# Second attention's gating and expert weights moved from VectorE to GpSimd, first attention's maxima transposed by VectorE

## The chip, the cores and the metric

The kernel runs on one core of a Trainium2 chip. TensorE (PE; PEld is its weight load), VectorE (DVE), ScalarE (ACT), GpSimd (POOL) and SyncE (SP, which here only issues DMAs) each run their own instruction list in order and meet at semaphores. The metric is the device time of one execution in microseconds, as the median of repeated runs.

## What is computed

`x` is [32, 256, 128] in float32, 8192 tokens. Layer 0 adds a latent attention with 16 heads and a top-1 mixture of 8 experts. Layer 1 adds a second attention (16 heads; a local window of 32, a remote part over 64 pooled latents, each scaled by a gate) and a mixture of 64 experts, top 8, with a shared expert.

```python
xn = _layernorm(x)
x = x + _L0_attn_ref(xn, ...) + _L0_ffn_ref(xn, ...)
xn = _layernorm(x)
x = x + _L1_attn_ref(xn, ...) + _L1_ffn_ref(xn, ...)

# _L0_attn_ref: a softmax over causal scores of width 36
scores = jnp.einsum('bhtl,bsl->bhts', q, Wdkv) / sqrt(d_head)
attn = jax.nn.softmax(jnp.where(causal, scores, -inf), axis=-1)
# _L1_attn_ref: the gates
gl = jax.nn.sigmoid(jnp.einsum('bhsd,hd->bhs', Q, gate_local_w))[..., None]
gr = jax.nn.sigmoid(jnp.einsum('bhsd,hd->bhs', Q, gate_remote_w))[..., None]
out = gl * local + gr * rem
# _L1_ffn_ref: the weights of the experts
w, idx = jax.lax.top_k(softmax(x @ gate_w), 8)
w = w / jnp.sum(w, axis=-1, keepdims=True)
shared = shared * jax.nn.sigmoid(x @ shared_gate_w)
```

## The kernel before

Each engine's list is written by hand, and the order of the calls is the order of the work. A batch is 256 tokens; there are 32, numbered by pair and half, and buffers alternate by half. The stages follow one another: the first attention (to about 830 us of the profile), the top-1 experts (to 985), the second attention and the routing (to 1600), the 64 experts.

First attention. One step handles the probabilities of batch b, the maxima and queries of the next batch n, and the keys of m after that. `smax` on TensorE (L1786 to L1799) makes scores of n in bfloat16 only to find each row's maximum; `red` on VectorE (L904 to L908) reduces them into `mneg`, eight pairs of heads a batch. `mt` then turns `mneg` [128 tokens, 16 heads] into rows: two transposes on TensorE (L1805) into `bankA`, a copy by ScalarE into `mT` (L1460), and two DMAs on SP that write `mT` into row 36 and row 100 of `qT` (`maxima`, L358 to L362), so that the real score matmul `st` (L1815, L1818) subtracts the maximum itself. `st(b, 0)` waits for these DMAs. TensorE ends a step with `smax(n, 7)`, `av(b, 3)`, `mt(n)`, `kv(m)`, `qproj(m, 0)`, and opens the next with `outp` (L1845, L1847) and `st`. On SP `maxima` stands ahead of `denominators` (L364 to L386): `remainders<-yT` (L367), then, once it has landed, `dq<-remainders` (L369). VectorE inverts `dq` (`invert`, L912) between `red(n, 0)` and `red(n, 1)`.

Second attention. One step handles the softmax and result of b, the projection and routing of n, the layer norm of m, and the combination of p, the batch before b. VectorE's order (`step1`, L1301) is: `pool_latents(n)` (L1216, `xp`), `shift(b,1)`, `combine(p)` (L1289 `at1`, L1291 `at2`, L1293 `aT`), `turn(b,0)`, `shift(b,2)`, `finish(p)`, `turn(b,1)`, `route(n)` (L1226 to L1234), `sums1(m)`, `shift(b,3)`, `turn(b,2)`, `mean1(m)` (L1211, `mv`), `turn(b,3)` (L1264), `weigh(n)` (L1240 to L1247), `shared_gated(b)` and `shared_hidden(b)` (L1270, L1275, into `shT`), `invert1(b)` (L1279), `shift(n,0)`, `turn_rows(b)` (L1283, `rowsT`). ScalarE goes from `xt1` (L1557, `xT`) over `keys(n)` (L1571 to L1575), `latent_keys(n)` (L1590 to L1595) and the exponentials (L1552) to `attended(b)`, which copies `rows` out of PSUM (L1634 to L1639). GpSimd adds the layer-0 experts to the stream and normalises (`stream1`, `norm1`), divides the rows (`normalise_rows`, L818), adds the residual (L786) and gathers rows for a later batch (L767). TensorE ends a step with `attend(b, 2)`, `attend(b, 3)`, `scores(n, 0)`, `shared_down(b)` (L2115), `scores(n, 1)`, `xt1(m)` (L2021) and `remote(b)` (L2107), which reads `rowsT`, and opens the next with `qk(n)` (L2030).

Of the kernel before, what the change touches and what calls it, by code (L numbers as in the profile page):

```python
# [9 lines left out]
ALU = mybir.AluOpType  # L10
ACT = mybir.ActivationFunctionType
AX = mybir.AxisListType
P = 128
NEG = -1e30
# [3 lines left out]
class Batch:  # L18
# [8 lines left out]
    def before(self):  # L27
        return Batch(self.pair, 0) if self.half == 1 else Batch(self.pair - 1, 1)

# [4 lines left out]
def program(nc, a, out):  # L34
# [27 lines left out]
    with ctx:  # L62
# [112 lines left out]
        mneg = sb("mneg", [P, 2, 2, 2, PAIRS])  # L175
        mT = sb("mT", [H, 2, T])
# [39 lines left out]
        lg1 = sb("lg1", [P, 2, E1 + 1])  # L216
        mx8 = sb("mx8", [P, 2, 8])
        lgr = sb("lgr", [P, 2, E1])
        mb = sb("mb", [P, 2, 2, E1], BF16)
        shl = sb("shl", [P, 2, E1])  # L220
        exl = sb("exl", [P, 2, E1])
# [77 lines left out]
        names = """consts zeroed zeroed1 w_a w_in x_in0 x_in1 x_in2 x_in3 bn stats_done var rstd_done xn_done xn_got xnT_ps  # L299
        xt_ps xt_act xt_dve rk_sb scats xnT_sb kv_ps kv_sb  # L300
        q_ps q_sb s_ps red_done mT_ps mT_sb st_ps exp_done av_done y_sb den_out den_in rec_done rec_out zrows_in z_done out_ps xa_done cst dumped passed xs_zero rt ex0 rk_ps staged scat0 scat1 te_done xs_in0 xs_in1 w1_sb xsT_ps xsT_sb h_ps h_act h_dve
# [3 lines left out]
        sh1_done sh_sb shd_ps av_ps rd_done rows_turned rem2_ps v_out v_in0 v_in1 rows_sb gate_ps gate_sb comb aT_done scaled x1_copied ao_ps r1_done res_done  # L305
        tab_out0 tab_out1 res_out0 res_out1 l1_consts wprep xpr_sb slots cnt_out cnt_in0 cnt_in1 owner_done picked_ps sel sidx_done tokf_done diag_done row_done same_done first_done mg_done ym_sb xg_in0 xg_in1 
# [20 lines left out]
        def _(sp):  # L327
# [82 lines left out]
            sp.dma_start(gw[:, 0:E1], a["L1_ffn_gate_w"]).then_inc(S["w1_in"], 16)  # L410
            sp.dma_start(gw[:, E1:E1 + 1], a["L1_ffn_shared_gate_w"]).then_inc(S["w1_in"], 16)
# [122 lines left out]
        def _(pool):  # L534
# [74 lines left out]
            def layer1_masks(g):  # L609
# [7 lines left out]
                if g == 3:  # L617
                    pool.memset(maskl[:, 0, 0:W], NEG).then_inc(S["l1_consts"], 1)
                    pool.wait_ge(S["l1_consts"], 1)
# [150 lines left out]
            def stream1(n):  # L770
# [6 lines left out]
                pool.wait_ge(S["x1_done"], n.b * 2 + 1)  # L777
# [17 lines left out]
            def norm1(n, prior):  # L795
# [5 lines left out]
                pool.wait_ge(S["x1_done"], n.b * 2 + 2)  # L801
                passed(pool)
                pool.tensor_copy(tab[:, u, :, 0:C], xa_all[:, bass.ds(n.b * 2, 2), :]).then_inc(S["x1_copied"], 1)
                deviation(n)
                pool.wait_ge(S["x1_copied"], n.b + 1)
# [15 lines left out]
            gather(Batch(0, 0))  # L821
            gather(Batch(0, 1))
            clear()
            stream1(Batch(0, 0))
            norm1(Batch(0, 0), False)
            stream1(Batch(0, 1))
            norm1(Batch(0, 1), False)
            gather(Batch(1, 0))
            with pool.Fori(0, LOOP - 1) as i:
                for b in (Batch(i, 0), Batch(i, 1)):  # L830
                    stream1(b.next().next())
                    norm1(b.next().next(), True)
                    normalise_rows(b)
                    add_stream(b)
                    gather(b.next().next().next())
            stream1(Batch(LOOP, 0))
            norm1(Batch(LOOP, 0), True)
            normalise_rows(Batch(LOOP - 1, 0))
# [42 lines left out]
        def _(dve):  # L881
# [140 lines left out]
            def step(n, p, q, staged, prior=True):  # L1022
# [20 lines left out]
                if n:  # L1043
                    red(n, 7)
# [1242 lines left out]
```

## Time and profile before

| | us |
|---|---|
| median of 3 runs | 1768.62 (1762.4 to 1772.06) |
| the profiled execution | 1777.13 |
| its span | 1774.3 |

| engine | busy us | share of the span |
|---|---|---|
| PE | 1545.6 | 87% |
| VectorE | 1153.1 | 65% |
| ScalarE | 1004.9 | 57% |
| GpSimd | 833.2 | 47% |

The span is cut into 40 slices of 44 us on the profile's page. TensorE shows 9 tenths or more in nearly all slices up to 830 us, and VectorE shows 9 tenths from 1020 to 1600 us. The granted TensorE clock is at full speed in both attentions and falls to 6 to 7 tenths at the end.

### The profile page before, as it was taken

The page shows a single profiled execution, that of the slowest core. Times are in us where ns is not written, and L with a number is a line of the kernel's source. Part 1 is how long each engine was busy: PE and PEld are TensorE (multiplying, and loading weights), DVE is VectorE, ACT ScalarE, POOL GpSimd, SP SyncE. Part 2 cuts the span into 40 slices and gives each one's busy share as a digit, 9 for nine tenths or more (in the row PEclk, how much of TensorE's full clock was granted, in tenths as well). Part 3 has the DMA queues.
Part 4 walks back from the last instruction along what each step waited for, and adds up shares of the span by engine and source line. Part 5 has one row for each costly group of instructions (what it writes and reads, how often), then busy time and mean ns, then how long its engine had stood idle before and what let it go on. Part 6 is the DMA issues. An engine that isn't in the chain of part 4 may idle for free.

```text
span 1774.3 us, 44513 instructions
## 1 busy us (share of the span) xinstructions
PE 1545.6 (87%) x14114; PEld 1125.7 (63%) x14115; DVE 1153.1 (65%) x2767; ACT 1004.9 (57%) x2558; POOL 833.2 (47%) x1415
## 2 busy tenths in 40 slices
PE   4798999999999999998998588888888888875883
PEld 4655555555555555555998477777777777764672
DVE  3355555555555555543554499999999999986661
ACT  3344555555555555543332578888788887862331
POOL 5233555555555555554443544444444444412663
PEclk9998999999999999999999599999999999996666
DMA  7402222222222222223332121111211212116444
GB/s 194 131 17 66 55 55 55 55 55 55 55 55 55 55 55 55 55 58 71 70 71 58 23 46 41 42 44 43 44 39 42 44 43 44 39 34 123 85 84 116
DMA packets 237550, 107.52 MB, mean 61 GB/s; under 512 B 141625, under 2 KB 225914, under 8 KB 237434
## 3 DMA queue, kind: packets, MB, share of 16 engines
q1 hardware_dynamic: 227258, 93.23, 21.9%
q0 software_dynamic: 10240, 13.64, 3.6%
q8 instruction: 27, 0.44, 0.1%
q14 instruction: 25, 0.20, 0.0%
HBM read 61.92 MB, written 40.16 MB: 58 GB/s over the span
## 4 chain that ended last, share of the span: by engine, by line
PE 49%; DVE 21%; issue 12%; DMA 6%; ACT 4%; SPq 3%; POOL 2%; DVEq 1%; POOLq 0%; another core or an unknown queue 0%; ACTq 0%
PE bankB L1832 7%; PE bankA L1780 5%; DVE mxs L1254 5%; DVE pt L1264 5%; PE bankT L1815 5%; PE bankT L1967 4%; PE bankB L1836 3%; PE bankS L1793 3%; PE bankT L1818 2%; PE bankB L2115 2%; DMA remainders<-yT 2%; PE bankS L1956 2%; PE bankT L1956 2%; PE bankB L1845 2%; DMA dq<-remainders 2%
## 5 line engine op out<-in xcount | busy, mean ns | idle before, releaser
L667 POOL TENSOR_SCALAR_AFFINE_SELECT probs<-probs 128x512 f32<-128x512 f32 x256 | 183.2, 739 | 167.0 <-ACT probs L1464 167.0
L906 DVE TENSOR_REDUCE mneg<-bankS 128x2 f32<-128x256 f32 x256 | 107.6, 420 | 227.2 <-PE bankS L1798 196.5
L1464 ACT ACTIVATE probs<-bankT 128x1024 f32<-128x1024 f32 x128 | 131.0, 1023 | 189.9 <-PE bankT L1818 189.9
L907 DVE TENSOR_REDUCE mneg<-bankS 128x2 f32<-128x512 f32 x256 | 174.6, 682 | 0.0
L1455 ACT ACTIVATE qT<-bankA,bd 128x256 f32<-128x256 f32 x256 | 107.5, 473 | 91.7 <-PE bankA L1780 91.7
L1780 PE MATMUL bankA<-xnT,wd 128*128 128x256 f32 x512 | 151.2, 420 | 0.0
L1815 PE MATMUL bankT<-qT,kT 37*128 37x512 f32 x512 | 140.0, 623 | 7.5 <-DMA qT<-mT 5.7
L660 POOL CAST qb<-qT 128x256 bf16<-128x256 f32 x256 | 97.2, 398 | 100.7 <-ACT qT L1455 100.5
L1832 PE MATMUL bankB<-probs,vaug 128*64 128x512 f32 x512 | 141.5, 631 | 1.1 <-ACT yT L1471 1.0
L1264 DVE STREAM_TRANSPOSE pt<-pe 128x768 f32<-128x768 f32 x128 | 123.7, 966 | 0.9 <-ACT pe L1552 0.9
L1471 ACT COPY yT<-bankB 128x512 f32<-128x512 f32 x128 | 75.0, 586 | 85.4 <-PE bankB L1836 85.4
L1780 PEld LDWEIGHTS bankA<-xnT,wd 128*128 128x128 f32 x512 | 90.8, 197 | 38.1 <-issue 30.4
L1552 ACT ACTIVATE pe<-pr 128x768 f32<-128x768 f32 x128 | 108.1, 845 | 10.4 <-DVE pr L1258 6.5
L2086 PE MATMUL bankT<-vx,pt 128*64 128x68 f32 x1024 | 72.1, 227 | 42.0 <-ACT gkm L1595 42.0
L1818 PEld LDWEIGHTS bankT<-qT,kT 37*128 37x128 f32 x512 | 51.1, 192 | 63.1 <-issue 63.1
L1793 PEld LDWEIGHTS bankS<-rowneg,rowsel 64*128 64x128 bf16 x1024 | 36.2, 95 | 84.7 <-issue 45.5
L2086 PEld LDWEIGHTS bankT<-vx,pt 128*64 128x64 f32 x1024 | 55.3, 136 | 54.4 <-ACT gkm L1595 27.5
L1836 PEld LDWEIGHTS bankB<-probs,vaug 128*64 128x64 f32 x512 | 37.6, 140 | 75.5 <-issue 66.5
L767 POOL DMA_INDIRECT yg<-ys_sorted,idx_g x64 | 67.2, 1049 | 36.9 <-POOL gate_g L763 26.7
L1793 PE MATMUL bankS<-rowneg,rowsel 64*128 64x128 bf16 x1024 | 74.9, 223 | 10.6 <-DVE mneg L907 6.8
L730 POOL COPY probs<-wall 128x516 f32 x72 | 44.8, 623 | 77.2 <-DVE qT L1138 74.3
L1818 PE MATMUL bankT<-qT,kT 37*128 37x256 f32 x512 | 79.0, 386 | 0.0
(316 smaller groups left out, 4301.9 us busy)
## 6 DMA issues: line engine op xcount, KB each, us to landing
rzb<-reciprocals SPq DMA_DIRECT2D x128, 128.0 KB
yT<-yT SPq DMA_DIRECT2D x64, 128.0 KB
xtab<-tab SPq DMA_DIRECT2D x32, 192.0 KB, 2.0
xs_sorted<-zeros SPq DMA_DIRECT2D x1, 4608.0 KB, 18.6
qT<-xs_sorted SPq DMA_DIRECT2D x144, 32.0 KB, 1.8
ys_sorted<-qT SPq DMA_DIRECT2D x36, 128.0 KB, 1.9
value_rows<-vrow SPq DMA_DIRECT2D x32, 128.0 KB, 1.8
vx<-value_rows SPq DMA_DIRECT2D x256, 16.0 KB, 1.8
```

Source lines behind the costliest of these rows:

```text
L667: pool.affine_select(out=blocks, in_=blocks, compare_op=ALU.is_ge, fill=0.0, base=0, pattern=[[0, 4], [1, P]], channel_multiplier=-1).then ...
L906: dve.tensor_reduce(mneg[:, n.half, 0, :, j], bankS[:, :, 0:128], AX.X, ALU.max, negate=True)
L907: dve.tensor_reduce(mneg[:, n.half, 1, :, j], bankS[:, :, 128:384], AX.X, ALU.max, negate=True).then_inc(S["red_done"], 1)
L1264: dve.transpose(pt[:, g].rearrange("p k b g q -> p (k b g q)"), pe1[:, g % 2].rearrange("p k s q -> p (k s q)")).then_inc(S["tr_done"], 1)
L1464: act.activation(pT[:, g % 2].rearrange("p e j t -> p e (j t)"), bankT[:, 0:2, :], ACT.Exp, scale=SCALE0).then_inc(S["exp_done"], 1)
L1552: act.activation(pe1[:, g % 2].rearrange("p k s q -> p s k q"), pr[:, g % 2, :].rearrange("p (s k q) -> p s k q", k=2, q=W), ACT.Exp, scal ...
L1780: ins = pe.matmul(bankA[:, k * T:(k + 1) * T], wd[:, 2 * r + k, :, :].rearrange("p e l -> p (e l)"), xnT[:, n.half, :], start=True, stop=True)
L1793: pe.matmul(blocks, rowsel[HALVES[e], k, :], rowneg[HALVES[e], k, :].unsqueeze(1).to_broadcast([LP, 2, LP]), start=(k == 0), stop=False, s ...
L1815: pe.matmul(bankT[:, e, :], kT[KEYS[e], u, 0:P], qT[KEYS[e], u, 2 * g:2 * g + 2, :].rearrange("p j t -> p (j t)"), start=True, stop=True, ...
L1818: ins = pe.matmul(bankT[:, 2 + e, 0:T], kT[KEYS[e], u, P:T], qT[KEYS[e], u, 2 * g:2 * g + 2, P:T], start=True, stop=True, skip_group_check ...
L1832: pe.matmul(bankB[HALVES[e], :], vaug[:, u, 0, :], pT[:, g % 2, e].rearrange("p j t -> p (j t)"), start=True, stop=False, skip_group_check ...
L2086: pe.matmul(slots_ps[DL * k:DL * (k + 1), n, 0:PW], pt[:, g, 1, k, 2 * (n % 2):2 * (n % 2) + 2, :].rearrange("p g q -> p (g q)"), vx[:, u, ...
```

## The change

It takes `mt` off TensorE and ScalarE: VectorE transposes `mneg` in blocks of 32 by 32 right after `red(n, 7)`, and SP writes the result into `qT` with four DMAs (32 partitions of 128 bytes each) in place of two (8 partitions of 1 KB each). In the second attention VectorE's product for `at1` goes to GpSimd (`open_gate`, `local_gate`), and so do the mask product, the scaling of the shared gate and the final weights (`weigh`, `weights`). VectorE keeps the sum of the weights, over the eight largest logits that now sit behind the 64 in `lg1`, `shl` and `exl`. VectorE's `shift(b, 3)` goes ahead of `sums1(m)`. `pool_latents` is not touched; VectorE pools the latents before and after. Left out below: renamed semaphores and the same order in the opening and closing steps.

```diff
-        mneg = sb("mneg", [P, 2, 2, 2, PAIRS])
-        mT = sb("mT", [H, 2, T])
+        mneg = sb("mneg", [P, 2, 2, PAIRS, 2])
+        mT = sb("mT", [P, 2, 2 * H])
...
-        lg1 = sb("lg1", [P, 2, E1 + 1])
+        lg1 = sb("lg1", [P, 2, 1 + E1 + 8])
...
             def maxima(n):
                 sp.wait_ge(S["mT_sb"], n.b + 1)
-                for e in range(2):
-                    r = LP * e + L
-                    sp.dma_start(qT[r:r + 1, n.half], mT[PAIRS * e:PAIRS * (e + 1), n.half, :]).then_inc(S[f"m_in{n.half}"], 16)
+                for k in range(P // W):
+                    sp.dma_start(qT[L:LP + L + 1:LP, n.half].rearrange("e j (t k q) -> e (j t) k q", t=2, q=W)[:, :, k],
+                                 mT[W * k:W * (k + 1), n.half, :]).then_inc(S[f"m_in{n.half}"], 16)
...
+            def local_gate(b):
+                pool.wait_ge(S["gate_up"], b.b + 1)
+                pool.wait_ge(S["rows_turned"], b.b + 1)
...
+                pool.tensor_tensor(at1[:, :], tg[:, b.half, 0, :], rowsT[:, 0:T], ALU.mult).then_inc(S["local_done"], 1)
+
+            def open_gate(b):
+                gate = tg[:, b.half, 0, :]
+                pool.wait_ge(S["gate_sb"], b.b + 2)
...
+                pool.tensor_scalar(gate, gate, 1.0, None, ALU.add).then_inc(S["gate_up"], 1)
+
+            def weigh(n):
+                u = n.half
+                pool.wait_ge(S["ex_done"], n.b + 1)
+                pool.wait_ge(S["M_done"], n.b + 1)
...
+                pool.tensor_scalar(sgc[:, u, :], tsg[:, :], 0.5, 0.5, ALU.mult, ALU.add)
+                pool.tensor_tensor(exl[:, :, 0:E1], exl[:, :, 0:E1], mb[:, u], ALU.mult).then_inc(S["rstep"], 1)
+
+            def weights(n):
+                u = n.half
+                pool.wait_ge(S["rstep"], n.b + 1)
+                pool.wait_ge(S["wsum_done"], n.b + 1)
...
+                pool.tensor_tensor(tab[:, u, :, C:C + E1], exl[:, :, 0:E1], wsum[:, 1, :].unsqueeze(2).to_broadcast([P, 2, E1]),
+                                   ALU.mult).then_inc(S["tab_done"], 1)
+
+            def step1(b, n, m, k):
+                if m:
+                    stream1(m)
+                    copy1(m, True)
+                if n:
+                    weigh(n)
+                if m:
+                    norm1(m)
+                if n:
+                    weights(n)
+                if b:
+                    open_gate(b)
                     normalise_rows(b)
                     add_stream(b)
...
+                if b:
+                    local_gate(b)
+                if k:
+                    gather(k)
...
+            def turn_maxima(n, prior):
+                dve.wait_ge(S["red_done"], n.b * PAIRS + PAIRS)
...
+                dve.transpose(mT[:, n.half, :], mneg[:, n.half].rearrange("p e j t -> p (e j t)")).then_inc(S["mT_sb"], 1)
...
+            def weight_sum(n):
                 dve.wait_ge(S["ex_done"], n.b + 1)
...
+                dve.tensor_reduce(wsum[:, 0, :], exl[:, :, E1:E1 + 8], AX.X, ALU.add).then_inc(S["top8"], 1)
+                dve.wait_ge(S["top8"], n.b * 2 + 2)
+                dve.reciprocal(wsum[:, 1, :], wsum[:, 0, :]).then_inc(S["wsum_done"], 1)
...
             def turn_rows(b):
                 dve.wait_ge(S["scaled"], b.b + 1)
+                if not b.opens():
+                    dve.wait_ge(S["local_done"], b.b)
...
             def combine(b):
                 u = b.half
                 dve.wait_ge(S["gate_sb"], b.b + 2)
-                dve.wait_ge(S["rows_turned"], b.b + 1)
-                dve.scalar_tensor_tensor(at1[:, :], tg[:, u, 0, :], 1.0, rowsT[:, 0:T], ALU.add, ALU.mult).then_inc(S["comb"], 1)
                 dve.wait_ge(S["rem2_ps"], b.b + 1)
                 dve.scalar_tensor_tensor(at2[:, :], tg[:, u, 1, :], 1.0, rem_ps, ALU.add, ALU.mult).then_inc(S["comb"], 1)
-                dve.wait_ge(S["comb"], b.b * 2 + 2)
+                dve.wait_ge(S["comb"], b.b + 1)
+                dve.wait_ge(S["local_done"], b.b + 1)
                 dve.tensor_tensor(aT[:, :], at1[:, :], at2[:, :], ALU.add).then_inc(S["aT_done"], 1)
...
+                if b:
+                    shift(b, 3)
                 if m:
                     sums1(m)
                 if b:
-                    shift(b, 3)
                     turn(b, 2)
...
                 av(b, GROUPS - 1, True)
-                if n:
-                    if m:
-                        pe.wait_ge(S["xnT_sb"], m.b + 1)
-                    mt(n)
                 if m:
+                    pe.wait_ge(S["red_done"], n.b * PAIRS + PAIRS)
                     kv(m)
-                    pe.wait_ge(S["mT_sb"], n.b + 1)
                     qproj(m, 0)
```

## Rows read from the trace of the kernel before

**Rows 1.** Stretches: length, busy PE, PEld, DVE, ACT, POOL, granted clock, DMA, GB/s.
```profile
132.00:734.00 602.00, 589.49 (x4601) 340.37 (x4598) 326.25 (x678) 321.75 (x581) 301.76 (x527) 0.99 0.21 56
1026.00:1581.00 555.00, 483.05 (x6000) 404.54 (x6000) 529.39 (x1137) 452.11 (x1381) 256.40 (x409) 1.00 0.20 43
```

**Rows 2.** Timeline of a first-attention step: start, length, engine, line, operation.
```profile
441.34 0.68 DVE L907 TENSOR_REDUCE mneg<-bankS 128x2 f32<-128x512 f32 x1
...
442.41 0.39 PE L1805 MATMUL bankA<-ident,mneg 128*16 128x128 f32 x2
...
442.63 0.60 PE L1771 MATMUL bankS<-xnT,lw 128*128 128x256 f32 x2
...
443.38 1.38 SPq L362 DMA_DIRECT2D qT<-mT  x2
...
444.89 0.73 SPq L367 DMA_DIRECT2D remainders<-yT  x2
...
446.70 0.30 PEld L1815 LDWEIGHTS bankT<-qT,kT 37*128 37x128 f32 x4
```

**Rows 3.** Chain that ended last, first attention: start, length, what.
```profile
243.56 0.35 SPq L367
243.96 2.68 DMA remainders<-yT
246.65 2.29 DMA dq<-remainders
```

**Rows 4.** Who waited for whom, TensorE, 200 to 700 us: total, times, longest.
```profile
PE bankS L1793 <- DVE mneg L907: 3.4, 19, 0.3
```

**Rows 5.** SP's DMA instructions by line: minimum, median, maximum in ns.
```profile
L362 SPq DMA_DIRECT2D qT<-mT x64: 626/654/703, 93.6 to 806.0; - x64
...
L374 SPq DMA_DIRECT2D yT<-yT x64: 536/583/593, 126.3 to 830.9; - x64
```

**Rows 6.** The view of DMAs: kilobytes of each, median us from issue to landing.
```profile
vx<-value_rows SPq DMA_DIRECT2D x256, 16.0 KB, 1.8
```

**Rows 7.** Chain that ended last, an opening step of the first attention.
```profile
121.05 1.90 DMA qT<-mT
```

**Rows 8.** Timeline of a second-attention step, VectorE.
```profile
1205.57 0.96 DVE L1264 STREAM_TRANSPOSE pt<-pe 128x768 f32<-128x768 f32 x1
1206.45 0.25 DVE L1240 TENSOR_TENSOR exl<-exl,mb 128x128 f32<-128x128 f32 x1
...
1207.67 0.67 DVE L1270 SCALAR_TENSOR_TENSOR shT<-tsh,bankA 128x512 f32<-128x512 f32 x1
...
1211.15 0.57 DVE L1283 STREAM_TRANSPOSE rowsT<-rows 128x384 f32<-128x384 f32 x1
...
1214.22 0.42 DVE L1289 SCALAR_TENSOR_TENSOR at<-tg,rowsT 128x256 f32<-128x256 f32 x1
```

**Rows 9.** The same step, the other engines.
```profile
1207.10 1.57 POOL L809 TENSOR_SCALAR tab<-tab,mv,rstd 128x128 f32<-128x128 f32 x2 [0.21 <-POOL rstd L793]
1210.04 0.85 POOL L818 TENSOR_TENSOR rows<-rows,recd 128x384 f32<-128x384 f32 x1 [1.38 <-ACT rows L1639]
...
1211.77 0.71 PE L2107 MATMUL bankT<-rowsT,wro 128*128 128x128 f32 x4 [0.19 <-DVE rowsT L1283]
1212.32 1.03 PE L2030 MATMUL bankB<-xT,wqk 128*128 128x256 f32 x4
...
1213.38 0.37 ACT L1571 COPY qs<-bankB 128x256 f32<-128x256 f32 x1 [0.36 <-PE bankB L2030]
```

**Rows 10.** Who waited for whom in the second attention, 1026 to 1562 us: TensorE, GpSimd.
```profile
PE bankT L2086 <- ACT gkm L1595: 39.6, 29, 1.6
...
POOL rstd L791 <- DVE mv L1211: 124.9, 29, 4.4
```

**Rows 11.** Groups of GpSimd's instructions by line: busy us, mean ns, idle before.
```profile
L786 POOL TENSOR_TENSOR res<-res,xa_all 128x256 f32<-128x256 f32 x32 | 23.2, 726 | 11.0 <-ACT res L1623 10.8 <-issue 0.2
...
L775 POOL TENSOR_SCALAR yg<-yg,gate_g 128x128 f32<-128x128 f32 x64 | 38.3, 601 | 54.5 <-DMA yg<-ys_sorted,idx_g 54.5
```

More of the change, by code:

```diff
@@ L28, in before, with opens @@
         return Batch(self.pair, 0) if self.half == 1 else Batch(self.pair - 1, 1)
+    def opens(self):
+        return type(self.pair) is int and self.b == 0
     def two_before(self):
@@ L819, in normalise_rows @@
                                    ALU.mult).then_inc(S["scaled"], 1)
[L821 to L832, printed above, removed]
+            def local_gate(b):
+                pool.wait_ge(S["gate_up"], b.b + 1)
+                pool.wait_ge(S["rows_turned"], b.b + 1)
+                if not b.opens():
+                    pool.wait_ge(S["aT_done"], b.b)
+                passed(pool)
+                pool.tensor_tensor(at1[:, :], tg[:, b.half, 0, :], rowsT[:, 0:T], ALU.mult).then_inc(S["local_done"], 1)
@@ L845, in _ @@
-            normalise_rows(Batch(LOOP, 0))
-            add_stream(Batch(LOOP, 0))
-            normalise_rows(Batch(LOOP, 1))
-            add_stream(Batch(LOOP, 1))
+                if b:
+                    local_gate(b)
+                if k:
+                    gather(k)
+            first, second = Batch(0, 0), Batch(0, 1)
+            gather(first)
+            gather(second)
+            clear()
+            stream1(first)
+            copy1(first, False)
+            norm1(first)
+            step1(None, first, second, Batch(1, 0))
@@ new lines, in _ @@
+            step1(first, second, Batch(1, 0), Batch(1, 1))
+            step1(second, Batch(1, 0), Batch(1, 1), Batch(2, 0))
+            with pool.Fori(1, LOOP - 1) as i:
+                step1(Batch(i, 0), Batch(i, 1), Batch(i + 1, 0), Batch(i + 1, 1))
+                step1(Batch(i, 1), Batch(i + 1, 0), Batch(i + 1, 1), Batch(i + 2, 0))
+            step1(Batch(LOOP - 1, 0), Batch(LOOP - 1, 1), Batch(LOOP, 0), Batch(LOOP, 1))
+            step1(Batch(LOOP - 1, 1), Batch(LOOP, 0), Batch(LOOP, 1), None)
@@ L1075, in _ @@
             red(first, 7)
+            turn_maxima(first, False)
             best()
@@ L1082, in _ @@
                     onehot(j + 1)
+            turn_maxima(second, False)
             kv(Batch(1, 0))
@@ L1326, in step1 @@
                 if n:
-                    weigh(n)
+                    weight_sum(n)
                 if b:
@@ L1511, in _ @@
             xnt(second)
-            mt(first)
             qevac(second, 0)
@@ L1656, in step1 @@
                     values(n, b is not None)
-                    route(n)
+                    route(n, b is not None)
                 if b:
@@ L1799, in smax @@
                 ins.then_inc(S["s_ps"], 1)
-            def mt(n):
-                pe.wait_ge(S["red_done"], n.b * PAIRS + PAIRS)
-                passed(pe)
-                for t in range(2):
-                    ins = pe.transpose(bankA[0:H, t * P:(t + 1) * P], mneg[:, n.half, t].rearrange("p e j -> p (e j)"), ident[:, :])
-                ins.then_inc(S["mT_ps"], 1)
             def st(b, g, prior):
```

120 lines of the change are left out of this document (54 added, 66 removed).

## The prediction

> **What bounds the kernel now.** I read the busy time by stretch first, then the waits, then the timeline of one step in each attention, following what each engine waited for. In the first attention TensorE is busy 98% of the time at full clock [rows 1]; in the second VectorE is busy 95% and TensorE 87% [rows 1]. Both shares mislead.
>
> First attention. The step in rows 2 is 22.27 us long; steps run to 22.4 on average. TensorE's only wait is that `smax(n, 2)` waits for `red(n, 1)`, 19 times in 22 steps, 3.4 us in all, 0.18 us each [rows 4]. Behind it stands SP: the maxima's DMAs, `remainders<-yT`, 2.68 us in flight, `dq<-remainders`, 2.29 us, then `invert`, which VectorE runs ahead of `red(n, 1)` [rows 3]. So two chains are level within 0.2 us: TensorE's own work, and SP's chain, which starts when the maxima are turned.
>
> Second attention. The step is 18.45 to 18.5 us. VectorE runs from `turn(b,3)` at 1205.57 to `turn_rows` at 1211.15 without a gap [rows 8]. TensorE's `remote` waits for `rowsT` (0.19 us), `qk` follows it, and ScalarE's `qs` waits for `qk` [rows 9]. From `qs` ScalarE runs on to `gkm`, for which TensorE's `attend` waits 29 times [rows 10]; TensorE then runs on to the end of `attend(b,3)`, ScalarE copies `rows`, GpSimd divides them, and `turn_rows` needs that. GpSimd ends at 1210.89 (1210.04 + 0.85, itself released by ScalarE's rows) and `turn_rows` starts at 1211.15 [rows 8, 9]. This is the number that matters most: only 0.26 us after its operand is there does VectorE reach the instruction. In alternate steps of the timeline it is 0.30. VectorE is the last comer by a quarter of a microsecond, and behind it a second closed ring (`qs`, `gkm`, `attend`, `rows`, division, turn, `remote`, `qk`, `qs`) has nearly the same period.
>
> **The change part by part, second attention.** Off VectorE: `weigh` takes 1.22 us (1206.45 to 1207.67) [rows 8]. What stays is a sum over 16 elements and a reciprocal, about 0.35, so 0.87 goes. `at1` is 0.42 long [rows 8], 0.33 from start to start. `shift(b,3)` ahead of `sums1(m)` hides a gap of about 0.1 behind a long instruction. `shl` grows from 64 to 72 columns, 0.02 back. Sum 1.3 us off a VectorE step. Of this only `weigh` lies between `turn(b,3)` and `turn_rows`: VectorE would reach `turn_rows` 0.87 earlier, but its operand is only 0.26 to 0.30 early, less about 0.04 for a release (`turn_rows` ended at 1211.72, `remote` began at 1211.77 [rows 8, 9]). The gain is 0.22 to 0.26 us a step; the rest becomes VectorE idling at `turn_rows` and before `turn(b,3)`, where it waits for ScalarE's last exponential. Some 29 steps: 7 us.
>
> This holds if GpSimd's division still starts when `rows` come. Ahead of it now stand `weights` and `open_gate`. `norm1` ended at 1208.67 and the division began at 1210.04, 1.37 us later [rows 9]; and since VectorE now has time over, `mean1`, for which GpSimd waits (124.9 us in 29 steps [rows 10]), comes up to 0.7 us earlier in the ring, so there are 1.4 to 2.0 us. `weights` is a product of 128 columns: 0.73 for 256 [rows 11] gives 0.4 to 0.5. `open_gate` adds a constant to 256 columns, a form the trace does not show at this size; below it stands half the 0.73 of the two-input product, above it the 0.60 for 128 columns with a pointer scalar doubled, 1.2 [rows 11]. I take 1.0, from the nearer form. Together 1.4 to 1.5: it fits, barely at the upper end without the earlier `mean1`. `weigh` (0.7) falls into the 4.4 us in which GpSimd waited for `mean1` [rows 10]. `local_gate` (0.73 by `res` [rows 11]) waits for `turn_rows`; queued behind it is `gather`, whose rows are then some 0.5 us later, against 2 us in which `x1_done` is early. `aT` needs `at1` only after `shift(b,1)` and `at2`, over 2 us after `turn_rows`; no cost. `tab` is saved 1.3 us later; SP is then still issuing value rows. No cost.
>
> **First attention.** Off TensorE: `mt`, 0.22 us from its start at 442.41 to `kv` at 442.63 [rows 2]. Off ScalarE a copy that hid. On VectorE a transpose of 32 columns, 0.2 by the slope between 384 columns (0.57) and 768 (0.96) [rows 8], plus 0.16 for the wait on its own semaphore. `red` ends at 442.02 [rows 2], so `mT` is ready at 442.4 instead of 443.36; that is 0.95 earlier. Then SP issues four DMAs instead of two. With a cost c per issue, `remainders<-yT` starts at 442.41 + 4c + 0.13, before at 444.89 [rows 2]: later by 4c - 2.35. The pair L362 took 1.38, so c = 0.69; L374, the other copy from SBUF to SBUF and like the new ones from 32 partitions, has a median of 0.58, 0.60 from start to start [rows 5]. Smaller issues on this queue exist (0.36 for L367 [rows 2]). Bounds 0.36 to 0.69; I take 0.60, since L374 is the nearest form: later by 0.05. So SP's chain, which carries the step, stays where it was, and TensorE's 0.22 goes into its wait for `red(n,1)`, which grows from 0.18 to about 0.4. Steady gain between -0.05 and +0.05 a step, 0 us. In the opening steps `st` waited for the maxima themselves, and `mt` stood alone on the path: 1 to 1.5 us gained. The maxima for `st(b,0)`: last issue at 442.41 + 1.8, landing 1.90 later [rows 7], at 446.1, against 446.70 - 0.22 [rows 2]: in time. The 128-byte pieces: the `vx` DMAs move 64-byte pieces and land 1.8 us after issue [rows 6], so I add nothing. `normalise(p, 2)` is 0.3 later on VectorE, a microsecond before `outp` needs it.
>
> **Sum.** 7 + 1.3 = 8.3 us off 1777.13 of the profiled execution (span 1774.3). The median is 8.5 lower than that execution, with the same steps, so I take it from the median: 1760.3, say 1760.
>
> **Rivals.** A: the issues are cheap. At c = 0.49 or less SP's chain is 0.4 earlier and TensorE's work bounds: 0.18 + 0.22 = 0.4 us in each of some 28 steps, 11 us. For it: many issues on SP are near 0.4; against it: both copies between SBUF and SBUF. Time 1749, up to 1756 for c between.
>
> B: busy share is the bound. If the second ring had room, each step would lose the 0.8 that `weigh` takes from VectorE's path: 29 x 0.8 = 23 us, with 1.3 more 1744, with A 1733. Against it stands the 0.26 between GpSimd's end and `turn_rows`.
>
> C, slower than before: SP late. With c = 0.69, as for the very DMAs that are replaced, `remainders<-yT` starts 0.41 us later, `invert` blocks `red(n,1)`, and each of some 29 steps is 0.41 longer: +12, less 8.3 = +4, 1772. It decides above c = 0.59. Should short pieces also land late, `st(b,0)` stalls: the margin of 0.4 is used up, and each 0.3 beyond costs 9 us, to 1781. Here a rule bears: the Trainium skill (DMA: Bandwidth & Descriptors, Specifications) wants 512 bytes at least, since below that the engines read, modify and write. By that rule the four transfers land later than the two, and this rival gains; the trace speaks against it, with 1.8 us for 64-byte pieces [rows 6].
>
> D: GpSimd late. If `open_gate` and `weights` take over 2.0 us, or are held up by VectorE, the division starts late and the ring grows: 0.25 late undoes the gain (1767), 0.5 late gives 1774. That the change does less than it says is true of one part: `pool_latents` was VectorE's already, worth nothing.
>
> **How the numbers follow.** Forecast, 1755 to 1765: 0.42. A, 1746 to 1756: 0.22. B, 1733 to 1745: 0.08. C, 1765 to 1781: 0.18. D, 1764 to 1779: 0.10. 0.5% is 8.8 us and about what a measurement can tell: below 1759.8 faster, above 1777.4 slower. Faster: half of the forecast, A and B, 0.51. Slower: a third of C, a fifth of D, 0.08. Same: 0.41. The range 1745 to 1775 leaves out B and the far end of C, under 0.15.
>
> **What would show it.** Right: second-attention steps of 18.2 to 18.3 us; an idle VectorE before `turn_rows` (L1283 now), put down to GpSimd's rows, 0.5 us or more in every step; GpSimd's division still released by ScalarE's rows. In the first attention the step stays at 22.4, TensorE's wait for `mneg` at `smax` grows to 0.4, SP's four issues take about 2.4 us. Wrong: issues of 0.45 and a step near 22.0 (A); steps below 18.0 (B); TensorE waiting for the maxima's DMA in steady steps, or a step near 22.8 (C); the division released by GpSimd's own `open_gate` (D).

## The result, and the profile of the changed kernel

The changed kernel takes 1756.83 us, the kernel before 1767.78 (medians of 17 runs each): a ratio of 0.9934 with a 95% interval of 0.9916 to 0.9951, which is 11.7 us of the kernel before, with 8.7 to 14.9. The forecast was 1760, 8.3 us off. The profiled execution has a span of 1754.6 us. VectorE and ScalarE are a little less busy than before, GpSimd went from 833 to 914 us. The page, engines by busy time:

```profile
span 1754.6 us, 44705 instructions
PE 1519.9 (87%) x14050; PEld 1115.4 (64%) x14051; DVE 1143.6 (65%) x2671; ACT 993.8 (57%) x2526; POOL 913.6 (52%) x1575
```

By stretch (columns as in [rows 1]): the steady first attention, then the second. TensorE is 98.6% busy in the first. In the second VectorE's share is down a point, from 95 to 94%; the prediction had warned that this share misleads, and again it does.

```profile
170.00:770.00 600.00, 591.73 (x4637) 342.90 (x4637) 333.65 (x704) 321.00 (x567) 309.66 (x540) 1.00 0.21 55
1035.00:1545.00 510.00, 439.22 (x5601) 375.27 (x5600) 480.49 (x953) 419.39 (x1290) 315.75 (x533) 1.00 0.20 44
```

One step of the first attention, the instructions that answer [rows 2]. `turn_maxima` (L958) ends 0.45 us behind the last `red` (L950), the four issues take 2.25 us, and `remainders<-yT` (L369) starts 2.87 us behind that `red`; before it was 444.89 - 442.02 = 2.87 as well [rows 2]. `kv` (L1817) starts 0.30 behind the `red` where it was 0.61.

```profile
458.12 0.68 DVE L950 TENSOR_REDUCE mneg<-bankS 128x2 f32<-128x512 f32 x1
...
459.04 0.21 DVE L958 STREAM_TRANSPOSE mT<-mneg 128x32 f32<-128x32 f32 x1 [0.24 <-DVE mneg L950]
...
459.10 0.70 PE L1817 MATMUL bankS<-xnT,lw 128*128 128x256 f32 x2
459.28 2.25 SPq L363 DMA_DIRECT2D qT<-mT  x4
...
461.67 0.68 SPq L369 DMA_DIRECT2D remainders<-yT  x2
463.27 0.30 PEld L1854 LDWEIGHTS bankT<-qT,kT 37*128 37x128 f32 x4
...
464.81 0.57 SPq L371 DMA_DIRECT2D dq<-remainders  x1
...
466.97 0.35 DVE L962 RECIPROCAL rq<-dq 128x32 f32<-128x32 f32 x1 [0.79 <-DMA dq<-remainders]
```

TensorE's wait for `mneg` between 200 and 700 us, the answer to [rows 4] (total, times, longest): it did not grow. The number is rough: in the run with the second attention's part alone, whose first attention is that of before, it is 1.4 us in 8 times, against 3.4 in 19 before.

```profile
PE bankS L1839 <- DVE mneg L950: 2.9, 15, 0.3
```

One step of the second attention on VectorE, as [rows 8]. It now idles 0.49 us before `turn_rows` (L1334); before, it came there 0.26 us after its operand.

```profile
1211.82 0.94 DVE L1313 STREAM_TRANSPOSE pt<-pe 128x768 f32<-128x768 f32 x1
1212.69 0.13 DVE L1295 TENSOR_REDUCE wsum<-exl 128x2 f32<-128x16 f32 x1
...
1212.93 0.67 DVE L1319 SCALAR_TENSOR_TENSOR shT<-tsh,bankA 128x512 f32<-128x512 f32 x1
...
1217.18 0.58 DVE L1334 STREAM_TRANSPOSE rowsT<-rows 128x384 f32<-128x384 f32 x1 [0.49 <-POOL rows L823]
```

The same step on the other engines, as [rows 9]. GpSimd runs from `norm1` (L814) through `weights` (L853, 0.40) and `open_gate` (L838, 0.87) to the division (L823) with no gap, and the division starts 0.27 us after ScalarE's last copy of `rows` ended (1215.77 + 0.26 = 1216.03).

```profile
1215.77 0.26 ACT L1685 COPY rows<-bankT 32x128 f32<-32x128 f32 x1
...
1217.81 0.71 PE L2140 MATMUL bankT<-rowsT,wro 128*128 128x128 f32 x4 [0.73 <-DVE rowsT L1334]
...
1213.35 1.58 POOL L814 TENSOR_SCALAR tab<-tab,mv,rstd 128x128 f32<-128x128 f32 x2 [0.21 <-POOL rstd L795]
1214.90 0.40 POOL L853 TENSOR_TENSOR tab<-exl,wsum 128x128 f32<-128x128 f32 x1
1215.38 0.87 POOL L838 TENSOR_SCALAR tg<-tg 128x256 f32<-128x256 f32 x1
1216.30 0.85 POOL L823 TENSOR_TENSOR rows<-rows,recd 128x384 f32<-128x384 f32 x1
1217.10 0.72 POOL L788 TENSOR_TENSOR res<-res,xa_all 128x256 f32<-128x256 f32 x1
```

The waits between 1035 and 1545 us, as [rows 10]. TensorE's wait for `gkm` is 1.8 us a step, up from 1.4: TensorE is ready for `attend` and the ring is not. GpSimd's wait for `mean1` fell from 124.9 to 33.2. It waits for ScalarE's rows in only 13 steps of 28; in the others it reaches the division as they come, or late.

```profile
PE bankT L2119 <- ACT gkm L1639: 49.9, 28, 1.9
...
POOL rstd L793 <- DVE mv L1265: 33.2, 28, 1.3
...
DVE rowsT L1334 <- POOL rows L823: 14.2, 29, 0.7
POOL rows L823 <- ACT rows L1685: 3.4, 13, 0.5
```

**Where the time went.** The first attention's steady step (from `kv` to `kv`, 27 steps) fell from 22.41 to 22.29 us, 3.4 us in all. From the first `turn_rows` to the last it takes 561.1 us instead of 570.5: 9.4 us, with a step of 18.20 instead of 18.49. That is 12.8 against a measured 11.7, by executions whose totals scatter.

The two profiled executions differ by 19.7 us of span, more than that. Of the rest, 1.0 us lies between the two attentions and 1.3 behind the last `turn_rows`. The other 4.5 us lie before the fifth `kv` (169.34 us after the start, before 173.86), and this is not the change: in the kernel with only the first attention's part, which has the same code there, the fifth `kv` is at 174.18, and in all fourteen profiled executions it falls anywhere from 165.7 to 174.6. What differs is TensorE's pace. The first block of `st`, in the timelines of the changed kernel and of that one:

```profile
96.38 1.13 PE L1854 MATMUL bankT<-qT,kT 37*128 37x512 f32 x4
```

```profile
96.43 2.08 PE L1812 MATMUL bankT<-qT,kT 37*128 37x512 f32 x4
```

and the stretch from 90 to 100 us in each (length, busy PE, granted clock, DMA share, GB/s):

```profile
90.00:100.00 10.00, 9.17 (x54) 1.00 0.01 2
```

```profile
90.00:100.00 10.00, 9.39 (x41) 1.00 0.01 2
```

The same four matmuls take 1.13 or 2.08 us. That is nearly twice as long, as at the lower of TensorE's two levels (1.2 against 2.4 GHz), while the granted clock says 1.00 in both. In the slower execution the half rate lasts until 107 us, in the other until 96. So the total of a single execution can't be compared with another to better than 9 us; stretches of it can, and so can medians.

### The profile page after: what moved, and what is told of

It reads as the page before. It is cut to its first block and busy times, and to the rows that moved or that the text cites. A ratio compares the mean times of both kernels' runs of the same rounds, so it can differ in the third digit from the quotient of the medians.

```text
span 1754.6 us, 44705 instructions
## 1 busy us (share of the span) xinstructions
PE 1519.9 (87%) x14050; PEld 1115.4 (64%) x14051; DVE 1143.6 (65%) x2671; ACT 993.8 (57%) x2526; POOL 913.6 (52%) x1575
## 5 line engine op out<-in xcount | busy, mean ns | idle before, releaser
L950 DVE TENSOR_REDUCE mneg<-bankS 128x2 f32<-128x512 f32 x256 | 174.3, 681 | 0.0
L769 POOL DMA_INDIRECT yg<-ys_sorted,idx_g x64 | 65.6, 1026 | 36.7 <-POOL gate_g L765 26.5
L2000 PE MATMUL bankT<-wall,qT 128*128 x576 | 79.8, 282 | 0.1
## 6 DMA issues: line engine op xcount, KB each, us to landing
xs_sorted<-zeros SPq DMA_DIRECT2D x1, 4608.0 KB, 18.5
```

The costliest lines, as they stand in the source:

```text
L950: dve.tensor_reduce(mneg[:, n.half, :, j, 1], bankS[:, :, 128:384], AX.X, ALU.max, negate=True).then_inc(S["red_done"], 1)
```

## The experiments

Each is the changed kernel with the edit shown, unless it says otherwise. A time is the median of 4 to 12 runs, and a ratio compares it with the kernel before, run on the same chip at the same time. Different runs are best compared by their ratios and their steps.

### The two parts alone

The first run keeps the first attention's edits (`mneg`'s order, `turn_maxima`, four DMAs in `maxima`, `mt` gone) on the kernel before. The second keeps all others.

> Only the first attention's part of the change; the second attention is that of before. SP-chain theory: the four issues measured 0.56 us each in the trace of after, so remainders<-yT starts 4 x 0.56 - 2.35 = 0.11 us earlier than before; the steady step falls from 22.41 to about 22.30 us, 27 steps give 3.0 us, and the opening gives another 1 to 4 us: 4 to 7 us faster, near 1762. TensorE theory (only the 0.22 us of the transposes taken off TensorE counts): 6 us from the steps, 1760. If the first attention's part is worth nothing, as the prediction had it for the steady steps: 1766. Second attention steps stay at 18.49 us.

Measured: 1765.1 us, ratio 0.9979 (0.9959 to 1.0000). First attention step 22.27 us, second attention step 18.50.

> Only the second attention's part of the change; the first attention is that of before. Both theories of the second attention: steps of 18.20 us instead of 18.49, 29 to 31 steps, 8 to 9 us faster, near 1759. First attention steps stay at 22.41 us. If the two parts add up, this ratio and that of the first attention's part alone make together the 0.9934 of the whole change.

Measured: 1760.27 us, ratio 0.9937 (0.9916 to 0.9959). First attention step 22.37, second 18.17. The parts add up: 3.7 and 11.1 us by the ratios, against 11.7 for both, within their intervals, and each moves only its own stretch. The first part is just below the 4 to 7 us expected; no gain of the opening is to be seen in the total: the fifth `kv` is at 174.18 with it, at 174.63 without.

### Taking each move back

at1 back on VectorE, with neither gate operation on GpSimd:

```diff
-                    open_gate(b)
                     normalise_rows(b)
                     add_stream(b)
-                    local_gate(b)
...
             def combine(b):
+                dve.scalar_tensor_tensor(at1[:, :], tg[:, u, 0, :], 1.0, rowsT[:, 0:T], ALU.add, ALU.mult).then_inc(S["comb"], 1)
```

> The changed kernel with at1 computed on VectorE again in combine, and neither open_gate nor local_gate on GpSimd. Ring theory (the prediction's: rows, division, turn_rows, remote, qk, qs, gkm, attend, rows carries the step and VectorE has slack): VectorE's 0.33 us between turn_rows and turn(b,3) are absorbed, GpSimd is lighter by 1.6 us, step 18.1 to 18.2, time 1754 to 1757. VectorE theory (in after VectorE runs without a gap from turn_rows to turn(b,3), and attend(b,3) starts 0.06 us behind it, so each 0.1 put there counts in full): step 18.5, 31 steps give 10 us, time 1766.

Measured: 1757.41 us, ratio 0.9940 (0.9915 to 0.9964); second attention step 18.14. VectorE does 0.33 us more and the step is 0.06 shorter. Moving at1 to GpSimd, a quarter of the change's relief for VectorE, gained nothing here.

The experts' weighing back on VectorE behind `turn(b, 3)`, and off GpSimd:

```diff
-                    weigh(n)
-                    weights(n)
...
+                dve.tensor_tensor(exl[:, :, 0:E1], exl[:, :, 0:E1], mb[:, n.half], ALU.mult).then_inc(S["rstep"], 1)
+                dve.tensor_reduce(wsum[:, 0, :], exl[:, :, 0:E1], AX.X, ALU.add).then_inc(S["top8"], 1)
+                dve.tensor_scalar(sgc[:, n.half, :], tsg[:, :], 0.5, 0.5, ALU.mult, ALU.add)
+                dve.tensor_tensor(tab[:, n.half, :, C:C + E1], exl[:, :, 0:E1], wsum[:, 1, :].unsqueeze(2).to_broadcast([P, 2, E1]),
```

> The changed kernel with the experts' weighing on VectorE again, behind turn(b,3), and off GpSimd. About 0.8 us more on VectorE between turn(b,3) and turn_rows, where VectorE now idles 0.5 us. Both theories: VectorE reaches turn_rows 0.3 us late, step near 18.5, time near 1766. If GpSimd were what bounds the step (the division late because of weights and open_gate), taking weights off it would give 0.4 us back ahead of the division, and the step would stay at 18.2 or fall.

Measured: 1761.52 us, ratio 0.9959 (0.9942 to 0.9975); step 18.39, not quite the 18.5 expected. `turn_rows` again comes late behind the division, by 0.08 to 0.33 us. So the weighing is the part that pays, 0.2 of the 0.29 us.

### Where the second attention's ring is tight

I followed the ring through ten traces, six of them of runs that come below. Times are means over some 25 steps between 1050 and 1530 us, counted from the start of `turn_rows` (the last column can differ by 0.01 from the step given in the text): the start of `qk` and of `qs`, the end of `gkm`, the end of `turn(b, 3)`, the start of ScalarE's copy of the sums (`dens`) behind `attend(b, 3)`, the end of its `rows`, the start of the division, and the next `turn_rows`.

```
                    qk    qs    gkm    turn3  dens   rows   divis. next
before              1.18  2.30  9.39   13.88  14.91  17.13  17.36  18.49
changed             1.19  2.31  9.40   13.74  14.83  17.05  17.32  18.21
at1 back            1.19  2.31  9.38   13.73  14.81  17.03  17.26  18.15
weighing back       1.18  2.29  9.38   13.80  14.87  17.09  17.32  18.41
open_gate twice     1.19  2.31  9.39   13.75  14.83  17.05  17.96  18.84
open_gate behind    1.19  2.31  9.40   13.73  14.82  17.04  17.27  18.15
spare product       1.19  2.31  9.41   13.75  14.83  17.05  17.28  18.16
qk first            0.40  1.57  8.67   13.67  14.71  16.93  17.21  18.09
three edits         0.45  1.61  8.69   13.36  14.40  16.62  16.85  17.73
all, at1 on GpSimd  0.45  1.61  8.74   13.10  14.16  16.38  16.61  17.50
```

The addition of `open_gate` done twice, the first time into a spare tile:

```diff
+                pool.tensor_scalar(spare[:, :], gate, 1.0, None, ALU.add)
                 pool.tensor_scalar(gate, gate, 1.0, None, ALU.add).then_inc(S["gate_up"], 1)
```

> The changed kernel with the addition of open_gate done twice on GpSimd (the first into a spare tile), 0.87 us more ahead of the division. If GpSimd has the 0.2 us of slack that its waits show in the trace of after, the division comes 0.6 to 0.7 us late in every step: step 18.85, 30 steps give 18 to 21 us more than the changed kernel, 1775 to 1778. If GpSimd had the room that the prediction gave it (0.5 us or more): step 18.5, time 1768 or less.

Measured: 1774.86 us, ratio 1.0040 (1.0020 to 1.0059); step 18.82. Of the 0.87 us added, 0.63 reach the step: GpSimd had 0.24 us of room ahead of the division. `open_gate` behind the division instead:

```diff
-                    open_gate(b)
                     normalise_rows(b)
+                    open_gate(b)
                     add_stream(b)
```

> The changed kernel with open_gate behind the division instead of ahead of it on GpSimd. Ring theory with GpSimd at its edge: GpSimd has 0.9 us of slack ahead of the division, which then starts 0.25 us behind ScalarE's rows in every step; the step falls from 18.20 to 18.10 or 18.15, 1.5 to 3 us, time 1754 to 1756. Theory that VectorE's slowed products matter as much: gather and copy1 are 0.9 us later still and meet mb and shift(b,3) instead of shl; shl returns to 0.30, mb stays at 0.5, step 18.0 to 18.1. If neither counts: 18.20.

Measured: 1752.1 us, ratio 0.9921 (0.9892 to 0.9950); step 18.14. Only 0.06 us a step, 2 us, was lost to its place ahead of the division; the interval is too wide to see that in the total, the step shows it. VectorE's two slow products, on which more below, are nearly gone in this run, and that shortened nothing further. `remote` behind `qk` on TensorE:

```diff
                 if n:
                     qk(n, b is not None)
+                if p:
+                    remote(p)
...
-                if b:
-                    remote(b)
```

> The changed kernel with TensorE's remote(p) moved behind qk(n): qk then no longer waits for turn_rows, only for the turned inputs. Ring theory: the closed ring (rows, division, turn_rows, remote, qk, qs, gkm, attend, rows) is cut open; qs can start up to 0.8 us earlier (when ScalarE is through with its exponential and xpr) and the next bound is VectorE's own 17.65 us of work: step 17.6 to 17.8 instead of 18.20, 30 steps give 12 to 18 us, time 1739 to 1745. If the ring is not what carries the step (VectorE from turn_rows to turn(b,3) without a gap, or GpSimd): step within 0.1 of 18.2, time 1754 to 1758.

Measured: 1752.2 us, ratio 0.9913 (0.9884 to 0.9941); step 18.07, not 17.7. `qk` comes 0.8 earlier and `gkm` 0.73 earlier, as expected, yet `dens` only 0.12. The table tells why: `dens` now starts 1.04 us behind the end of `turn(b, 3)`, and VectorE waits for no other engine between `turn_rows` and there. Two chains lay within 0.1 us of each other, and the second is VectorE's. In the kernel before this second chain was already the later one: there `dens` starts 1.03 us behind `turn(b, 3)` in each of 26 steps, which is the least that any trace shows. My expectation had counted VectorE's busy time (17.65) as its bound, although 0.49 us of its idling lie before `turn_rows`, behind `turn(b, 3)`, where they help nothing.

### VectorE's products beside GpSimd's

VectorE should have been 0.33 us lighter between `turn_rows` and `turn(b, 3)` than before, since at1 left, and yet with at1 back that way is no longer. The groups by line and shape, 1050 to 1540 us, show what ate it (busy us, mean ns, idle before), here of the kernel before:

```profile
L1234 DVE TENSOR_TENSOR mb<-lg,lgr 128x128 bf16<-128x128 f32 x27 | 7.9, 292 | 0.9
L1232 DVE TENSOR_TENSOR shl<-lg,mx 128x128 f32<-128x128 f32 x27 | 7.6, 281 | 0.0
```

of the changed kernel:

```profile
L1286 DVE TENSOR_TENSOR shl<-lg 128x144 f32<-128x144 f32 x27 | 17.9, 664 | 0.0
L1288 DVE TENSOR_TENSOR mb<-lg,lgr 128x128 bf16<-128x128 f32 x27 | 14.2, 525 | 0.9
```

and with at1 back on VectorE:

```profile
L1269 DVE TENSOR_TENSOR shl<-lg 128x144 f32<-128x144 f32 x27 | 8.1, 298 | 0.0
L1271 DVE TENSOR_TENSOR mb<-lg,lgr 128x128 bf16<-128x128 f32 x27 | 8.0, 296 | 0.9
```

The same two instructions take 1.19 us in the changed kernel and 0.59 without the gate operations on GpSimd. The timeline of the changed kernel has the reason: GpSimd's `stream1` and `copy1` lie beside them. Both come 0.6 us later behind `turn_rows` than before, since `gather` is queued behind `local_gate`.

```profile
1207.30 0.80 DVE L1286 TENSOR_TENSOR shl<-lg 128x144 f32<-128x144 f32 x1
1208.14 0.51 DVE L1288 TENSOR_TENSOR mb<-lg,lgr 128x128 bf16<-128x128 f32 x1
...
1207.21 0.72 POOL L782 TENSOR_TENSOR xa_all<-xa_all,yg 128x256 f32 x1 [0.27 <-POOL yg L777]
1208.11 0.39 POOL L805 COPY tab<-xa_all 128x256 f32 x1 [0.17 <-POOL xa_all L782]
```

To show that the overlap does it, and not the form of `shl`, the next run has at1 on VectorE and a product of two spare tiles in `local_gate`'s place:

```diff
+            def fill(b):
+                pool.wait_ge(S["rows_turned"], b.b + 1)
+                pool.tensor_tensor(spare[:, 0, :], spare[:, 1, :], spare[:, 2, :], ALU.mult)
```

> As the run with at1 back on VectorE, but in the place of local_gate GpSimd multiplies two spare tiles of the same size (0.73 us), so gather and with it stream1 and copy1 come 0.7 us later again, as in the changed kernel. Contention theory (while GpSimd's copy1 and stream1 run, VectorE's products with both operands in SBUF are slow: shl 0.66 us against 0.30, mb 0.53 against 0.30): both slow down again, shl to 0.6 or more and mb to 0.5, VectorE's way from turn_rows to turn(b,3) grows by 0.6 us of which ScalarE's exponential hides 0.2, step 18.4 to 18.5 against 18.14, time 1765 to 1768. If shl and mb are slow in the changed kernel for their own form (144 columns, another tile) or for open_gate: they stay at 0.30, step 18.14, time 1756.

Measured: 1756.99 us, ratio 0.9945 (0.9921 to 0.9968); step 18.15. `mb` is slow again, `shl` hardly, and its timeline shows that this is where the overlap fell: `shl` starts as GpSimd's product is nearly over, `mb` meets the copy.

```profile
L1280 DVE TENSOR_TENSOR mb<-lg,lgr 128x128 bf16<-128x128 f32 x27 | 13.6, 505 | 0.9
L1278 DVE TENSOR_TENSOR shl<-lg 128x144 f32<-128x144 f32 x27 | 9.2, 342 | 0.0
```

```profile
1203.39 0.33 DVE L1278 TENSOR_TENSOR shl<-lg 128x144 f32<-128x144 f32 x1
1203.76 0.51 DVE L1280 TENSOR_TENSOR mb<-lg,lgr 128x128 bf16<-128x128 f32 x1
...
1202.84 0.72 POOL L783 TENSOR_TENSOR xa_all<-xa_all,yg 128x256 f32 x1 [0.27 <-POOL yg L778]
1203.73 0.39 POOL L806 COPY tab<-xa_all 128x256 f32 x1 [0.17 <-POOL xa_all L783]
```

So the cause stands, but the price that I expected (0.3 us of step) fell away: 0.26 us more on VectorE left the step at 18.15. The waits between 1035 and 1545 us tell where it went (total, times, longest), with at1 back, with the spare product, and with `open_gate` behind the division:

```profile
DVE pt L1296 <- ACT pe L1578: 6.8, 28, 0.3
```

```profile
DVE pt L1305 <- ACT pe L1587: 0.3, 1, 0.3
```

```profile
DVE pt L1313 <- ACT pe L1596: 13.4, 28, 0.6
```

With at1 back VectorE waits 0.24 us a step for ScalarE's last exponential ahead of `turn(b, 3)`. The slow product of the spare run fills just this wait, and the other chain, `gkm` to `attend(b, 3)`, brings `dens` to 14.81 anyway. The run with `open_gate` behind the division says the same of the changed kernel: `gather` is later still there, so the product and the copy of `stream1` and `copy1` come behind VectorE's two products, and only `stream1`'s scaling lies beside them. The two are nearly as fast as before, yet VectorE now waits 0.48 us a step for the exponential and the step is 0.06 shorter.

```profile
L1286 DVE TENSOR_TENSOR shl<-lg 128x144 f32<-128x144 f32 x27 | 9.9, 367 | 0.0
L1288 DVE TENSOR_TENSOR mb<-lg,lgr 128x128 bf16<-128x128 f32 x27 | 7.9, 294 | 0.9
```

The Trainium skill (SBUF — State Buffer, Who interferes with whom) says that a VectorE instruction with two inputs in SBUF contends with a GpSimd instruction that reads SBUF, and that one with at most one does not, outside VectorE's two-port modes. The traces agree with it for GpSimd's product and copy: the two products slow down, the transposes and the reductions over `bankT` keep their time (0.97 and 0.94 us). They do not agree for every GpSimd instruction: in the kernel before, a VectorE product of two SBUF tiles lies wholly inside `norm1` on GpSimd (1207.10 to 1208.67 [rows 9]) in all 26 steps and takes 0.28 us in each.

```profile
1207.46 0.28 DVE L1247 TENSOR_TENSOR tab<-exl,wsum 128x128 f32<-128x128 f32 x1
```

What sets the two cases apart is not shown.

### The first attention's chain

The last of the four DMAs given out as two:

```diff
+                for e in range(2):
+                    sp.dma_start(rows_of[e:e + 1, :, 3], mT[W * 3 + 16 * e:W * 3 + 16 * e + 16, n.half, :])
```

> The changed kernel with the last of the four DMAs of the maxima given out as two (the same bytes), so five issues. SP-chain theory: remainders<-yT starts 0.5 us later, and with it dq, invert and red(n,1); first attention steps 22.7 instead of 22.29, 27 to 29 steps, 10 to 13 us slower than the changed kernel, 1767 to 1770. If TensorE's own work carries the step and SP has slack: 22.3, time 1757.

Measured: 1795.32 us, ratio 1.0161 (1.0134 to 1.0188); step 23.37. SP's DMAs in one step:

```profile
455.52 1.20 SPq L366 DMA_DIRECT2D qT<-mT  x2
456.84 0.74 SPq L371 DMA_DIRECT2D remainders<-yT  x2
460.24 0.58 SPq L373 DMA_DIRECT2D dq<-remainders  x1
```

One issue more costs 1.08 us a step, not 0.4. `remainders<-yT` starts 0.67 later behind `turn_maxima`, and it is then 3.40 us to `dq` where it was 3.14, so `invert` is 0.90 late. The ordinary steps are longer by just that, 0.89 us in the mean, and three of the 27 by another 1.6 to 1.8 us. That is the SP chain, and TensorE's own work is no bound in this range; why the remainders take longer on their way is open. Two of the four issues given to ScalarE, behind its last `yT`:

```diff
-                for k in range(P // W):
+                for k in range(P // W // 2):
...
+            def maxima(n):
+                act.wait_ge(S["mT_sb"], n.b + 1)
+                for k in range(P // W // 2, P // W):
+                    act.dma_start(qT[L:LP + L + 1:LP, n.half].rearrange("e j (t k q) -> e (j t) k q", t=2, q=W)[:, :, k],
+                                  mT[W * k:W * (k + 1), n.half, :]).then_inc(S[f"m_in{n.half}"], 16)
```

> The changed kernel with two of the four DMAs of the maxima issued by ScalarE, behind its last copy of yT, where it idles 1.34 us. SP-chain theory: remainders<-yT 1.1 us earlier, invert early, TensorE's wait for mneg (0.13 us a step) gone and TensorE's own work the bound: step 22.1 to 22.2 instead of 22.29, 3 to 5 us faster than the changed kernel, 1752 to 1754. If SP is not what bounds, or ScalarE's two issues hold up qevac: 22.3 or more, 1757 or more.

Measured: 1750.06 us, ratio 0.9912 (0.9896 to 0.9929); step 22.06, in turn 22.01 and 22.09. `remainders<-yT` starts 0.97 us earlier, but takes 3.52 us to `dq` instead of 3.14, so `invert` is only 0.62 earlier. That is enough: TensorE's wait for `mneg` is gone (200 to 700 us).

```profile
PE bankS L1848 <- DVE mneg L950: 0.3, 2, 0.2
```

### Together

at1 back on VectorE, `remote` behind `qk`, and the split issues:

> Three edits of this study together on the changed kernel: at1 back on VectorE and both gates off GpSimd, remote(p) behind qk(n) on TensorE, and two of the four DMAs of the maxima issued by ScalarE. First attention as in the run with the split issues: steps of 22.05 us. Second attention, contention theory: with qk free of turn_rows the step is what VectorE needs from turn_rows to turn(b,3) (12.46 us without slow products and without waiting for the exponential, 12.74 with slow products where remote stood behind qk alone and the step was 18.07) and 5.35 us behind it: 17.8 us, 30 steps give 12 us beside the 6 of the first attention, time 1739 to 1741. If the edits do not add up in the second attention: 18.1, time 1748.

Measured: 1733.83 us, ratio 0.9815 (0.9789 to 0.9841); steps 22.06 and 17.73. With `qk` first, VectorE's way to `turn(b, 3)` is the bound, and there the slow products counted: `turn(b, 3)` ends at 13.36 against 13.67, although at1's 0.33 us are back. So at1 on GpSimd costs in one order of the work and is free in another. The last run keeps at1 on GpSimd, with `open_gate` behind the division:

> The changed kernel with remote(p) behind qk(n), the maxima's DMAs split between SP and ScalarE, and open_gate behind the division; at1 stays on GpSimd, so against the run of three edits together only at1 (0.33 us from start to start) is off VectorE's way from turn_rows to turn(b,3). There VectorE had no gap. If VectorE carries the step now: 17.45 us against 17.73, 30 steps give 8 us, time 1726; with shl at 0.44 (slowed by GpSimd's late gather) 17.6 and 1730. If another chain is level with VectorE (ScalarE's or TensorE's), 17.7 and 1734, as in the run of three edits.

Measured: 1732.42 us against 1771.15, ratio 0.9791 (0.9761 to 0.9822); steps 22.06 and 17.50. Here `mb` takes 0.30 and `shl` 0.36 us, so most of at1's 0.33 is really off VectorE's way: `open_gate` behind the division has delayed `gather`, and with it GpSimd's product and copy, until behind them. 1726 to 1730 us were expected for that, and on the run before's base (1765.43) the ratio gives 1728.5. It is the fastest kernel of the study, though from the run before only the steps tell it apart (0.23 us).

## Why the prediction came out as it did

**Second attention, the bound.** Right. The prediction said that of 1.3 us of relief only 0.22 to 0.26 us a step would count, because a second ring lies behind VectorE. Measured: 0.29, and VectorE idles 0.5 before `turn_rows` (14.2 us in 29 steps). Rival B (0.8 us a step) is out. The parts, by the table: from the division to the next `turn_rows` 1.13 became 0.89 us, that is 0.24 and the predicted number; `dens` comes 0.08 earlier, which was not predicted; the division comes 0.04 later behind `rows`. The 0.08 contradict one sentence of the prediction, that of the relief only what lies between `turn(b,3)` and `turn_rows` counts: VectorE's way to `turn(b,3)` carried `dens` in every step before, and its 0.14 us counted until the other chain took over.

**What the prediction left out there.** It put the later `gather` at no cost, "against 2 us in which `x1_done` is early". Nobody waits for `stream1`, so far it held. But it looked only at who waits, and not at what would run beside it: `stream1` and `copy1` moved onto `shl` and `mb`, which cost VectorE 0.62 us, more than at1 had given (0.33). Besides, 0.31 us in which `pool_latents` waited for ScalarE's `xT` went, and about 0.1 by `shift(b, 3)` coming first: -0.33 - 0.31 - 0.1 + 0.62 = -0.12, and `turn(b, 3)` ends 0.14 earlier. The loss was hidden by the other chains, not absent: with the products nearly as fast as before (`open_gate` behind the division) the step is only 0.06 shorter, and once `qk` goes first they cost 0.3 us of step and more.

**GpSimd.** `weights` 0.40 (predicted 0.4 to 0.5), `open_gate` 0.87 (1.0 taken, bounds 0.37 to 1.2), `local_gate` 0.73, all near. "It fits, barely" was right for half the steps: the room is 0.24 us, and 0.06 us a step were lost. The division was released by ScalarE's rows in 13 steps of 28 only, not in all. One of the signs of being right, the division released by ScalarE's rows, thus held only in part. Rival D was near; with the operation doubled the division is 0.64 late and the time 1774.86, and D had 1774 for 0.5 late.

**First attention.** The term 4c - 2.35 was the right one, and c was 0.56, not 0.60, so -0.11 instead of +0.05. The prediction had put `mT` down as ready 0.38 us behind the last `red`. The measured start of `remainders<-yT` is unchanged though (2.84 and 2.86 us behind the last `red` in the mean over 24 steps), because `turn_maxima` begins 0.24 us after that `red` and ends at 0.45. `invert` is 0.10 us earlier behind that `red`, and the step 0.12 shorter, because `invert` follows `dq`'s issue after 2.10 us instead of 2.21; that this DMA is back sooner is seen, its cause is not. The predicted steady gain of 0 was 3.4 us, a term of the sum that nothing in the prediction foresaw. TensorE's wait for `mneg` was 2.9 us in 22 steps, 0.13 each, instead of growing to 0.4. That SP's chain carries the step is shown from both sides: one issue more costs 1.08 us, two less give 0.23, and then TensorE, with 0.3 us of waits for `mneg` left in 500, is the bound. The gain of 0.4 that rival A promised if issues were cheap was 0.35 (22.41 to 22.06), when the chain was really shortened.

**The opening.** 1 to 1.5 us were predicted, and 0.35 are there. From the end of the last `red` to the `st` that follows it takes 3.92 instead of 4.04 us in the first step, and 3.67 instead of 3.90 in the second, where `st` waits for the maxima's DMAs (1.14 us, before 1.24); in the third the wait scatters from 2.4 to 4.8 us between executions, with 3.7 and 4.1 where the code is that of before. The step that failed is "`mt` stood alone on the path": `mT` is ready almost a microsecond sooner, but `st` waits for the last DMA, and the change's own two extra issues stand in front of it. The prediction's own numbers had this: 442.41 + 1.8 against a second issue of the old pair that began near 444.1. In the total nothing of it can be seen, since TensorE's rate scatters the opening by 9 us.

**The sum.** 7 + 1.3 + 0 = 8.3 was predicted. By the traces it is 9.4 + 0.35 + 3.4 = 13.2, by the measurement 11.7 (8.7 to 14.9), so the predicted gain lies just below the interval. That the sum came as near as it did is partly luck: the opening was put too high by about 1 us and the steady steps too low by 3.4. Taking the median and not the profiled execution as the base was right: that execution was 4.5 us slower than the changed kernel's in its opening alone, for no reason of the change.

## What to carry to other kernels

Before work is moved off the busiest engine, look for how early the operand of its next waiting instruction is: the relief can't be worth more than what is level with it. When an instruction is queued ahead of others on GpSimd, look at what those will run beside, and not only at who waits for them; a VectorE product of two SBUF tiles took 0.66 us here instead of 0.30. And when two chains are level, shortening one shows little (0.13 us a step here) until the other is shortened too (0.57 more).

## What was not expected of the hardware

- VectorE's `shl` (0.30 us) took 0.66 and `mb` (0.29) 0.53 while GpSimd ran a product or a copy of SBUF tiles; GpSimd's own 0.73 and 0.39 us grew by less than 0.02. Beside GpSimd's `norm1` a product of 0.28 us stayed at 0.28.
- A block of the maxima's SP issues, divided by their number, is 0.56 us long with 32 source partitions, 0.60 with 16, and 0.69 for the old pair with 8 (from start to start 0.58, 0.59 and 0.74): fewer partitions are not cheaper. The old pair's pieces were also longer, 1 KB each.
- Four short DMAs ahead of it left `remainders<-yT` at 3.14 us to the next issue (before 3.15, behind the old pair), five made it 3.40. Two, with two more on ScalarE's queue, made it 3.52, so their number on SP is not what decides; what does is open.
- TensorE ran the same matmuls at half rate in the opening for up to 11 us longer in one execution than in another, with the granted clock at 1.00 in both.
